# Attention scores in 32x32 tiles, read from the masked keys, in an attention and GRU kernel on Trainium2

## What is computed

```python
# x: (128, 32, 256), cond: (128, 256), all float32
scale_shift = emb @ W_emb + b_emb                       # emb = cond
xn = rms_norm(x, g_norm) * (1.0 + scale) + shift
q, k, v = split_heads(xn @ W_qkv)                       # 16 heads of 16
q, k = rms_norm(q, g_q), rms_norm(k, g_k)
attn = softmax(q @ k.T * 16 ** (-0.5))                  # 32 x 32 for each sequence and head
x = x + (o + o @ W_out)                                 # o = attn @ v
h = cond
for t in range(32):                                     # GRU, one step for each token
    h = gru_cell(h, x[:, t])
    y[:, t] = x[:, t] + h
```

## Time and profile before

| | us |
|---|---|
| median of 3 runs | 342.06 (342.03 to 342.14) |
| span of the profiled execution, first to last instruction | 340.0 |
| scores of the first group start at | 25.67 |
| scores of the last group start at | 180.56 |
| first pass of the GRU's input products at | 191.54 |

### The profile page before, as it was taken

The page is one execution under the profiler, slowest core; times in us unless marked ns, Lnnn a source line. Parts: engine busy times, 40 slices in busy tenths (PEclk is TensorE's granted clock), DMA queues, the critical chain, the costliest instruction groups (busy, mean ns, idle before and its releaser), DMA issues.

```text
span 340.0 us, 12168 instructions
## 1 busy us (share of the span) xinstructions
PE 323.3 (95%) x4177; PEld 293.4 (86%) x4177; DVE 246.3 (72%) x665; ACT 238.0 (70%) x722; POOL 224.5 (66%) x404
## 2 busy tenths in 40 slices
PE   8988899899999999999986999999999999999994
PEld 8767788788888888888874999999999999999994
DVE  3778898888999999999996455565555556555555
ACT  4787777778888788889656566666666666666662
POOL 6787787867777877878778346555555555555542
PEclk9999999999999999999999999999999999999999
DMA  5965237742343333233332221111112111122221
GB/s 202 307 193 151 86 76 234 226 132 85 109 121 113 101 114 99 86 117 116 112 109 65 80 77 48 61 49 62 62 62 62 48 58 50 62 62 62 63 62 33
DMA packets 32205, 34.14 MB, mean 100 GB/s; under 512 B 5286, under 2 KB 26796, under 8 KB 32172
## 3 DMA queue, kind: packets, MB, share of 16 engines
q1 hardware_dynamic: 25868, 26.10, 25.6%
q10 hardware_dynamic: 6304, 7.61, 7.0%
HBM read 12.46 MB, written 8.39 MB: 61 GB/s over the span
## 4 chain that ended last, share of the span: by engine, by line
PE 78%; POOL 7%; SPq 4%; DMA 4%; issue 3%; DVE 3%; ACT 1%; POOLq 0%; DVEq 0%; ACTq 0%
PE bank L1287 38%; PE bank L1244 19%; PE bank L1400 4%; PE bank L1419 4%; PE bank L1388 4%; DMA operands<-operands 4%; PE bank L1531 3%; SPq L414 2%; POOL operands L485 2%; PE bank L1380 2%; SPq L405 2%; PE bank L1250 2%; PE bank L1371 2%; POOL xn L496 1%; POOL xn_lo L531 1%
## 5 line engine op out<-in xcount | busy, mean ns | idle before, releaser
L1287 PE MATMUL bank<-wih_lo,wo_parts 128*128 128x256 f32 x192 | 56.2, 294 | 0.0
L1287 PE MATMUL bank<-wih_hi,wo_parts 128*128 128x256 f32 x192 | 54.6, 285 | 0.2 <-POOL pair_lo L600 0.2
L1287 PE MATMUL bank<-wih_hi,pair_lo 128*128 128x256 f32 x192 | 52.8, 279 | 0.0
L1287 PE MATMUL bank<-wqkv_hi,hT_hi 128*128 128x256 f32 x192 | 52.5, 292 | 0.0
L611 POOL TENSOR_TENSOR operands<-operands,h 128x128 f32<-128x128 f32 x64 | 29.6, 462 | 34.2 <-ACT operands L932 33.4
L1287 PE MATMUL bank<-wqkv_lo,hT_hi 128*128 128x256 f32 x192 | 49.9, 279 | 0.0
L1187 DVE TENSOR_TENSOR operands<-bank,operands 128x128 f32<-128x128 f32 x64 | 18.6, 291 | 39.3 <-ACT operands L929 39.3
L1244 PE MATMUL bank<-wqkv_hi,xn_hi 128*128 128x512 f32 (+1 forms) x124 | 46.4, 375 | 0.2 <-POOL xn_lo L531 0.2
L618 POOL TENSOR_TENSOR w_emb_sb<-h,w_emb_sb 128x256 f32<-128x256 f32 x31 | 22.9, 737 | 30.7 <-DVE h L1204 30.7
L1287 PE MATMUL bank<-wqkv_hi,hT_lo 128*128 128x256 f32 x192 | 42.7, 279 | 0.0
L1244 PE MATMUL bank<-wqkv_hi,xn_lo 128*128 128x512 f32 (+1 forms) x124 | 41.9, 338 | 0.0
(11 more groups left out here) (138 smaller groups left out, 975.2 us busy)
## 6 DMA issues: line engine op xcount, KB each, us to landing
v_diag<-v_rows SPq DMA_DIRECT2D x124, 34.0 KB, 2.1
operands<-operands SPq DMA_DIRECT2D x32, 128.0 KB, 2.1
out_dram<-x ACTq DMA_DIRECT2D x16, 256.0 KB, 2.6
w_emb_sb<-out_dram SPq DMA_DIRECT2D x32, 128.0 KB, 2.1
operands<-operands SPq DMA_DIRECT2D x63, 64.0 KB, 2.0
out_dram<-w_emb_sb SPq DMA_DIRECT2D x31, 128.0 KB, 1.7
x_in<-in_x_dram SPq DMA_DIRECT2D x7, 512.0 KB, 8.6
stage_w<-in_L_cond_W_ih_dram ACTq DMA_DIRECT2D x2, 384.0 KB, 3.4
```

The source lines that it names most:

```text
L1287: return pe.matmul(dst, moved, gate_columns(weights, k, block), start=False, stop=True, skip_group_check=True)
```

## The change

- `k_diag`, its memset on DVE, the DMAs of `place_keys` (SP) and of `last_keys` (ACT) and their semaphores go. `operands` shrinks from 14 x 256 to 6 x 256 columns.
- `scores` reads `k_masked`. A matmul now has the 32 rows of one strip as weights and as contraction, and 64 columns (the even and the odd head's keys) as the moving operand: 32 matmuls for a group, so 64 passes. They are made in two halves, n = 0 with the strips 0 and 2, n = 1 with the strips 1 and 3. Both halves of a pair of strips write the same rows of the same bank, so between them PE waits for its own semaphore `s_half`, which the last matmul of the first half raises.
- `scores` waits for `k_masked_ready` in place of the DMAs, `mask_keys` for the scores of two groups before (`s_ps`) in place of them.
- All values are placed by SP, at turn v + 5, and the last load of x goes out after the values of groups 0 and 1.
- The stores of x2 go from ACT's queue to SP's, at turn o + 11 as before.
- `attention_products` picks its columns by another rule, since the heads stand in another order. As many matmuls, of the same shapes.
- No lag of a stage changes.

The diff, cut to what matters:

```diff
-        KD, KM = 2 * 2 * 2 * D, 2 * 2 * D
-        operands = sb("operands", [P, 14 * D])
-        k_diag = operands[:, 0:KD].rearrange("p (s n r j k) -> p s n r j k", s=2, n=2, r=2, k=T)
-        k_masked = operands[:, KD:KD + KM].rearrange("p (s r f) -> p s r f", s=2, r=2)
+        operands = sb("operands", [P, 6 * D])
+        k_masked = operands[:, 0:4 * D].rearrange("p (s r f) -> p s r f", s=2, r=2)
...
-            def place_keys(g, slot):
-                sp.wait_ge(k_masked_ready, g + 1)
-                strips = KEY_STRIPS[:-1] if isinstance(g, int) and g == NG - 1 else KEY_STRIPS
-                for i, (first, count) in enumerate(strips):
-                    rows = slice(PB * first, PB * (first + count))
-                    sp.dma_start(k_diag[rows, slot, i % 2, :, :, :].rearrange("p r j k -> p (r j k)"),
-                                 k_masked[rows, slot, :, :].rearrange("p r f -> p (r f)"))\
-                      .then_inc(k_diag_ready[slot], 16)
+            def store_results(o, slot):
+                sp.wait_ge(x2_ready, o + 1)
+                groups = out_groups[:, bass.ds(o - 1, 2), :] if not isinstance(o, int) else out_groups[:, o - 1:o + 1, :]
+                sp.dma_start(groups, x2[:, slot - 1:slot + 1, :]).then_inc(x2_stored[slot // 2], 16)
...
                 v = group(base, u, SP_V)
-                if v is not None and not (isinstance(v, int) and (v <= 2 or v >= NG - 3)):
+                if v is not None:
                     place_values(v, (u - SP_V) % 4)
...
-                if turn_is(base, u, SP_KEYS + 1):
+                if turn_is(base, u, SP_V + 1):
                     load_x(4 * FIRST_SPREAD, NG, x_loaded[FIRST_SPREAD])
+                o = group(base, u, SP_X2)
+                if o is not None and (u - SP_X2) % 2 == 1:
+                    store_results(o, (u - SP_X2) % 4)
...
             def mask_keys(k, slot):
                 pool.wait_ge(qkT_ready, k + 1)
                 if later(k, 2):
-                    pool.wait_ge(k_diag_ready[slot], spread(k - 2, slot, len(KEY_STRIPS)))
+                    pool.wait_ge(s_ps, k - 1)
...
-            dve.memset(operands[:, 0:KD], 0.0).then_inc(k_diag_clear, 1)
...
             def scores(g, slot):
-                pe.wait_ge(k_diag_ready[slot], spread(g, slot, len(KEY_STRIPS)))
+                pe.wait_ge(k_masked_ready, g + 1)
                 if later(g, 1):
                     pe.wait_ge(logits_ready, g)
                 pe.sem_inc(scores_clear, 1)
-                for c in range(KC):
-                    for b in range(GB):
-                        for i in range(2):
-                            rows = slice(2 * PB * i, 2 * PB * i + 2 * PB)
-                            last = pe.matmul(s_tiles[i][T * b:T * b + T, c * P:c * P + P]
-                                             .rearrange("p (r n k) -> p n r k", r=2, k=T),
-                                             qkT[rows, slot, c * P + T * b:c * P + T * b + T],
-                                             k_diag[rows, slot, :, :, GB * c + b, :], start=True, stop=True)
-                last.then_inc(s_ps, 1)
+                for n in range(2):
+                    if n == 1:
+                        pe.wait_ge(s_half, g + 1)
+                        pe.sem_inc(scores_clear, 1)
+                    for c in range(KC):
+                        for b in range(GB):
+                            for i in range(2):
+                                rows = slice(2 * PB * i + PB * n, 2 * PB * i + PB * n + PB)
+                                columns = slice(c * P + T * b, c * P + T * b + T)
+                                dst = s_tiles[i][T * b:T * b + T, c * P:c * P + P]\
+                                    .rearrange("p (r n k) -> p n r k", r=2, k=T)[:, n, :, :]
+                                last = pe.matmul(dst, qkT[rows, slot, columns], k_masked[rows, slot, :, columns],
+                                                 start=True, stop=True)
+                    last.then_inc((s_half, s_ps)[n], 1)
```

More of the change, by code:

```diff
@@ L30 @@
 NB = P // PB
-KEY_STRIPS = ((0, 1), (1, 2), (3, 1))
 BANK = 512
@@ L43 @@
 POOL_XN, POOL_KEYS, POOL_OT, POOL_XLO, POOL_NEWTON = 3, 6, 10, 3, 1
-SP_V, SP_KEYS = 5, 6
+SP_V, SP_X2 = 5, 11
 UNROLL = 4
@@ L245, in adaptive_attention_gru @@
         xhat_free = sem("xhat_free")
+        s_half = sem("s_half")
         s_ps = sem("s_ps")
@@ L297, in later @@
             return not isinstance(g, int) or g >= n
-        def spread(g, slot, parts):
-            return (g - slot) * (8 * parts) + 16 * parts
         def spread_by_four(g, slot, parts):
@@ L402, in place_values @@
                 sp.wait_ge(v_ready, v + 1)
-                for b in range(2 if isinstance(v, int) and v in SHARED_VALUES else GB):
+                for b in range(GB):
                     rows = slice(T * b, T * b + T)
@@ L407, in place_values @@
                       .then_inc(v_diag_ready[slot], 16)
[L409 to L426 removed]
+            out_groups = out.rearrange("(g b) t d -> (b t) g d", b=GB)
+            def store_results(o, slot):
+                sp.wait_ge(x2_ready, o + 1)
+                groups = out_groups[:, bass.ds(o - 1, 2), :] if not isinstance(o, int) else out_groups[:, o - 1:o + 1, :]
+                sp.dma_start(groups, x2[:, slot - 1:slot + 1, :]).then_inc(x2_stored[slot // 2], 16)
+            def body(base, u):
                 v = group(base, u, SP_V)
[L428 removed]
+                if v is not None:
                     place_values(v, (u - SP_V) % 4)
[L430 to L433 removed]
+                if turn_is(base, u, SP_V + 1):
                     load_x(4 * FIRST_SPREAD, NG, x_loaded[FIRST_SPREAD])
[L436 removed]
+                o = group(base, u, SP_X2)
+                if o is not None and (u - SP_X2) % 2 == 1:
+                    store_results(o, (u - SP_X2) % 4)
+            pipeline(sp, body, NG - 1 + SP_X2)
             for stored in x2_stored:
@@ L692, in load_gate_weights @@
                 act.dma_start(staged[:, i % KC, :], source[(i % KC) * P:(i % KC) * P + P, :]).then_inc(loaded[i % KC], 16)
-            def place_values(v, first, last):
-                act.wait_ge(v_ready, v + 1)
-                for b in range(first, last):
-                    rows = slice(T * b, T * b + T)
-                    act.dma_start(v_diag[rows, v % 4, b, :, :].rearrange("p h f -> p (h f)"),
-                                  v_rows[rows, v % 4, :, :].rearrange("p h f -> p (h f)"))\
-                       .then_inc(v_diag_ready[v % 4], 16)
-            def last_keys():
-                act.wait_ge(k_masked_ready, NG)
-                first, count = KEY_STRIPS[-1]
-                rows, slot = slice(PB * first, PB * (first + count)), (NG - 1) % 2
-                act.dma_start(k_diag[rows, slot, (len(KEY_STRIPS) - 1) % 2, :, :, :].rearrange("p r j k -> p (r j k)"),
-                              k_masked[rows, slot, :, :].rearrange("p r f -> p (r f)")).then_inc(k_diag_ready[slot], 16)
             def gate_weights(c):
@@ L768, in last_pair_columns @@
                          p_x2T.rearrange("p (c b t) -> p c t b", c=KC, b=GB)[:, :, 0:2, :]).then_inc(pair_hi_ready, 1)
-            out_groups = out.rearrange("(g b) t d -> (b t) g d", b=GB)
-            def store_results(o, slot):
-                act.wait_ge(x2_ready, o + 1)
-                groups = out_groups[:, bass.ds(o - 1, 2), :] if not isinstance(o, int) else out_groups[:, o - 1:o + 1, :]
-                act.dma_start(groups, x2[:, slot - 1:slot + 1, :]).then_inc(x2_stored[slot // 2], 16)
             def queries_keys(g, slot):
@@ L897, in body @@
                     first_state()
-                for v in SHARED_VALUES:
-                    if turn_is(base, u, v + ACT_V):
-                        place_values(v, 2, GB)
                 for i in range(4):
```

17 lines of the change are left out of this document (2 added, 15 removed).

## The result

The kernel after the change takes **350.47 us** (median of 4 runs, 349.93 to 351.24) against 342.10 us of the kernel before on the same chip: a ratio of 1.0233, 95% interval 1.0198 to 1.0269. It is slower, by some 8 us. The span of its profiled execution is 348.1 us, 8.1 more than before.

What follows compares the result with a forecast made beforehand. PE was taken to bound the attention's middle. 28 turns of 0.43 us lose 12.0 us; the DMAs return 4.1 us early and 1.5 at the end, together 5.6: +6.4 us on 342.06, 348.5 us, range 345.1 to 353.0.

Steps and rivals of the forecast that it cites:

- What bounds: Middle of the attention: PE has no idle time in a 5.05 us turn, so its own work sets the turn.
- A half takes 0.24: Scores after the change: each half's 32 passes take 0.24 us from first to last.
- a set's time is its columns: Inside a half: a set of eight passes takes 0.055 us for 64 columns, against 0.11 for 128.
- The gap between the halves, 0.40: PE's wait for its own signal: 0.40 us from last pass to next first pass, 0.31 as lower end.
- c: Extra time of the scores in a turn: 0.43 us, counted in groups 1 to 28, 12.0 us lost.
- What the DMAs give back, 4.1 us: Early and later turns where PE's scores waited for the k_diag DMAs: 4.1 us regained.
- The end, 1.5 us: Last maxima on DVE start at 179.82, behind a transpose, in place of 181.32; all that follows keeps this 1.5 us.
- What costs nothing: The memset, the stores and values on SP's queue, and less DMA traffic: no effect on the time.
- The sum: Whole kernel: 12.0 us lost less 5.6 regained, +6.4 us, for 348.5 us.
- The wait almost free: Rival at the gap between halves: 0.15 us, 0.17 more in a turn, 341.2 us; chance 6%.
- Issue sets the pace: Rival in the scores: 32 passes take 0.40 us whatever their columns, 0.74 more in a turn, 357.7 us; chance 12%.
- The floor of some 25 ns between starts: Harsher rival in the scores: matmul starts never under about 25 ns apart, a half 0.8 us, 380 us; no separate chance.

Runs made afterwards that it cites:

- no_wait: Kernel after, but the second half of the scores reads the first half's strips, so no wait stands between; odd strips' scores not computed: 341.99 us, ratio 0.9991.
- four_masks_64: Kernel before without the DMAs, keys masked four ways, and each 64-row scores matmul cut into two of 64 columns, no wait: 342.73 us, ratio 1.0006.
- before_with_wait: Kernel before, with only a wait of PE for its own semaphore added in the middle of its 16 scores matmuls: 354.84 us, ratio 1.0378.
- stores_on_act: Kernel after, with the stores of x2 issued on ACT's queue again, as before: 350.04 us, ratio 1.0232.
- four_masks: Kernel before's 16 scores matmuls without the DMAs or a wait; keys masked four ways, three by POOL, one by ACT: 338.61 us, ratio 0.9884.
- values_between: Kernel after, with the products with the values put between the two halves of the scores: 345.21 us, ratio 1.0085.
- dmas_kept: Kernel before with the scores of the kernel after, wait included; the DMAs to k_diag still run and are waited for: 357.80 us, ratio 1.0437.

## Why the prediction was right, and where it was not

The direction, the mechanism and the range held; the time was 2.0 us under the measured one. Step by step:

- **What bounds.** Right. PE had no slack in the middle of the attention, and every turn grew by what the scores grew.
- **A half takes 0.24.** Measured 0.238 and 0.243. The reason behind it, that a set's time is its columns however many sets follow, holds for 32 passes in a row alone (no_wait, four_masks_64). Without the wait the forecast of the scores would have been 0.18 too low, so the second half's 0.24 came out in part by luck.
- **The gap between the halves, 0.40.** Mis-sized: 0.455. It was put together from DVE's start behind a pass, a correction for the shorter pass, and PE's waking. The correction was 0.03, not 0.05, if the rows of the tile make no difference (before_with_wait), which makes 0.02 of it; the other 0.035 lie in the signal or the waking, and the runs don't tell which. c became 0.48 in place of 0.43, and 27 turns of 0.05 ahead of group 28 are 1.4 us.
- **What the DMAs give back, 4.1 us.** Right. With 27 x 0.43 lost the scores of group 28 should have been 7.5 later; with 1.4 for the gap and 0.19 for group 8's stall it is 9.1. They start at 177.09, 8.98 later.
- **The end, 1.5 us.** From 8.98 at group 28 to 7.71 at the last maxima, 1.27 came back where 1.1 was expected (1.5 less one more c), and the maxima follow a transpose without idle time, as said. Wrong was "all that follows hangs on these maxima, so it keeps this". From there to the first GRU pass 0.6 was lost again. The chain that ended last, in this stretch of the kernel after (start, us, what), and POOL's timeline in the kernel before:

```profile
190.16 1.37 POOL wih_lo L495 x2
191.53 0.53 issue
192.05 0.72 POOL oT_lo L502
```

```profile
180.72 1.98 POOL L515 TENSOR_TENSOR wih_lo<-stage_w,wih_hi 128x384 fp32r<-128x384 f32 x2
183.77 0.73 POOL L522 TENSOR_TENSOR oT_lo<-oT,oT_hi 128x256 fp32r<-128x256 f32 x1 [1.08 <-ACT oT_hi L813]
```

Before, POOL had split its gate weights by 182.70, then stood idle 1.08 us for ACT and made the low part of `oT` at 183.77, 2.45 behind the last maxima. After, the same gate weights (190.12, 1.97 us long) end at 192.09, and `oT_lo` starts at 192.05, 3.02 behind. POOL's queue became what comes last, the wait that the forecast should have looked for after it had taken the DMA away. This 0.57 is read from the traces alone; no run moved those instructions.
- **What costs nothing.** Right for the memset, the stores, the values and the traffic (stores_on_act; no wait of DVE or PE for them).
- **The sum.** 6.4 + 1.4 + 0.2 + 0.6 - 0.2 (1.27 in place of 1.1 at the end) = 8.4, against 8.1 in the span and 8.4 in the median.
- **The rivals.** The wait almost free: excluded by 0.455 and by before_with_wait. Issue sets the pace: not within a half; beyond 32 passes something other than the columns does, which no row of before could show, and what it is stays open. The floor of some 25 ns between starts, from the Trainium skill's page "TensorE: Matmul & The Clock Gate", section "Wait — 56ns, not 53.3ns?", does not bind here in any kernel: 32 passes start within 0.24 us, 8 ns apart, and even the slow ones of four_masks_64 are 12 ns apart.

## What to carry to other kernels

An engine that has no slack should not wait for its own result: on PE such a wait cost 0.3 to 0.46 us each time here. Other work that is ready by itself covers the wait, but the changes of shape around it cost too: 0.16 us a turn was left with the products in it, 0.36 with the projection. If that work waits for another engine, the second half is held up with it. To rid PE of a DMA, make the operand on engines that have room and leave PE's instructions as they are (four_masks), for twice the instructions at half the size are not free. When a wait goes at the head of a chain, read the next engine's queue as well: what it had idle is all that it can give. And before a small difference is explained, look at the granted clock of both traces: a single stretch of 3.41 us at 1.2 GHz went with 0.9 to 1.6 us more here.

## What was not expected of the hardware

- Float32 passes of 64 columns on eight tiles start 8 ns apart for the first 32 (0.24 us), and the next 32 some 12 ns apart (0.375 us), on tiles of 32 rows and of 64 alike. Behind a wait of 0.455 us the next 32 have the quick pace again (after), and so they have behind 32 passes of the products, without a wait (values_between).
- PE's wait for its own semaphore: 0.455 us from the start of the last pass to that of the next with 64 columns on 32 rows, 0.489 with 128 columns on 64 rows.
- Passes stall for 0.2 to 1.3 us with no releaser in eight of the nine traces with 64 passes for each group; in the kernel after both stalls came at the same instructions in two executions.
- The granted clock fell to 1.2 GHz for 3.41 or 6.8 us ahead of the GRU in four of the twelve traces (values_between, dmas_kept, before_with_wait, four_masks), each time within 1.5 us of the end of PE's wait for x, which was 1.55 to 2.20 us long there; the kernel before, with 1.54, kept 2.4 GHz. In dmas_kept it fell in the first turns as well. The same 83 passes took 8.50 us with such a stretch and 7.03 without.
